# Gate logits of both head halves in one matmul stage from the second batch on, the raw second half kept in SBUF, engine orders rewritten

## Chip, cores and metric

The kernel runs on one core of one Trainium2 chip. The metric is device microseconds (us) from start to end of one execution, as the median of several runs; less is better. In this core TensorE (PE in the profile) does the matmuls and transposes, VectorE (DVE), ScalarE (ACT) and GpSimd (POOL) the elementwise work, and SyncE (SP) issues DMAs. Each of the five works through its own list of instructions in order, and waits on semaphores that the others raise.

## Reference

The input x has 8 batches of 512 tokens of 128 channels. Each batch goes through a half-step feed-forward network (FFN), an attention with 16 heads of 64, and a second half-step FFN, each behind a layernorm and added to its input:

```python
x = x + 0.5 * ffn(layernorm(x)); x = x + attention(layernorm(x)); x = x + 0.5 * ffn(layernorm(x))
# attention, x of (8, 512, 128), H = 16, D = 64
q = rmsnorm((x @ Wq), q_rms_w); k = rmsnorm((x @ Wk), k_rms_w); v = x @ Wv
omega_eff = softplus(omega) * slopes
u_n = u / maximum(norm(u), 1e-6)
gate_logits = einsum('bthd,hd->bht', k, u_n) / sqrt(D)
gate = softplus(gate_logits)
bias = -dist * omega_eff[:, None, None] * gate[:, :, None, :]     # dist = max(i - j, 0), causal
attn = softmax(einsum('bihd,bjhd->bhij', q, k) / sqrt(D) + bias)
y = (attn @ v) @ Wproj
```

The FFN is 128 to 512 to 128 with an exact GELU, and its two weight matrices get a small addition made from the batch's own first tokens, so they are made anew for each batch. What the change is about is one number per token and head, the gate logit. It is linear in k before the RMS norm, so the kernel gets it from the layernormed tokens times a prepared matrix (wu, 128 channels by 16 heads) and divides by the RMS of k afterwards.

## The kernel before, in words

**Precision.** Most matmul operands are fp16 pairs, a high part and a low part. A product (`product`, L1121 to L1125) is three matmuls into one PSUM region: high by high, high by low, low by high.

**Order of the work.** All five engines are driven by one table, `ORDER`: for each engine a list of stages for the parts `lead`, `first` (batch 0), `body` (batches 1 to 6, one list used six times) and `final` (batch 7). A stage in the part of batch b belongs to batch b (THIS), to the one before (LAST) or to the one after (NEXT). So the part of batch b holds its attention beside the first FFN and the projections of the next batch and the second FFN of the one before. The order is written out by hand. Each engine runs its list strictly in order; `run` calls the function that belongs to the stage.

**PSUM.** Four of the eight banks form a ring (banks 4 to 7). Every PE stage takes one or more units of it in the order of PE's own list (`UNITS`: 3 for the max-scores of a head, 2 for two turned heads, 1 for most others, 1 for `gl`). `room` makes PE wait until the bank's last user is done (`work_taken`), `full` makes a reader wait for PE (`work_full`), `taken_by` marks the reader's last instruction as the one that frees the bank.

**The stages of a batch**, with their names in the table and the lines of the matmuls or of the main instruction:

- `zt` transposes z, the layernormed tokens; `ln1`, `ln2` are the layernorm's statistics and its normalization; `m`, `h`, `out` the FFN (weights, hidden, output), `"a"` for the first FFN and `"c"` for the second; `add` adds the FFN's result.
- `qk q t` projects queries and keys of a quarter of the heads (four heads, quarter q of 0 to 3) for token block t. ACT copies the result and its squares out of PSUM (L1007, L1006), DVE sums the squares (L1569), `qkn` is the inverse RMS on ACT (L1018) and the multiply with it on POOL (L878).
- `v j t` projects the values of half j; ACT takes the high part, DVE the low part (L1627).
- `gl hf` (`gate_logits`, L1213) is the gate logits of the eight heads of half hf, for all four token blocks: 4 products of 8 columns, 12 matmuls. There are two such stages per batch: `gl 0` stands after the projections of quarters 0 and 1, `gl 1` near the end of the part. On DVE `take_logits` (L1572) multiplies the bank by the inverse RMS of k (`rs`) into `lg`. On ACT `gate_softplus` (L1038, stage `gate`) takes four small activations of `lg`; it waits until the logits' bank is freed. On POOL `gates` (same stage name, L898) makes the two bias rows of each head from them, `gt`. On PE `gr hf` (`gate_rows`, L1224) turns `gt`, on DVE `take_gate_rows` (L1579, L1586) copies it to `gtt`, and on SP `gd` (`place_gates`, L749, L752) issues two DMAs per quarter that put it into rows of the fp16 operand `qk1`.
- `t p` turns the pair of heads p (L1236: eight fp32 transposes); ACT takes the high parts (L1059), DVE the low parts (L1595). SP places them with DMAs (`rows`, `swap`, `back`).
- `a h` (`max_scores`, L1240 to L1254) computes rough scores of head h, from which DVE takes the row maxima (L1605). It waits for the DMAs of the gate rows and the turned heads of its quarter. `nm q` turns the maxima of a quarter, ACT copies them, SP puts them into a row of `qk1`.
- `s h` (`scores`, L1264, L1280 to L1282) computes the scores, transposed, in banks 0 to 2; ACT takes the exponential (L1084). `pl h` on POOL makes its fp16 low part (L852). In batch 7 (`shared_heads`) DVE makes a share of the low parts (L1518).
- `pv h` (`weighted`, L1285) multiplies by the values in bank 3: 128x65 products, the 65th column being the sum; DVE divides by the sum (`over_sums`, L1616, L1620). `yt p` makes the high and low part of a pair's y on ACT and POOL (L856), and SP issues a transposing DMA; `wp i` projects y (the rows `ps<-wp_h,y_hl`), and DVE adds the attention (`add_attention`).

In the list of a body part the stretch around the seam to the next part is, on PE before: `out c`, `qk 3 3`, `a 5`, `pv 13`, `s 15`, `a 6`, **`gl 1`**, `pv 14`, `a 7`, `t 4`, `wp 2`, `nm 1`, `t 5`, `t 6`, and then in the next part `pv 15`, `t 7`, `s 0`, `v 1 0`, `v 1 1`, **`gr 1`**, `s 1`. The wait on `rs` in `take_logits` needs all four `qkn` of a half, and `qkn 3 1` is one of the last stages of the part, which is where `gl 1` stands.

The functions that the change touches:

Of the kernel before, what the change touches and what calls it, by code (L numbers as in the profile page):

```python
# [6 lines left out]
ALU = mybir.AluOpType  # L7
# [39 lines left out]
            ("s", 7, THIS), ("a", 12, THIS), ("v", 1, 3, THIS), ("pv", 6, THIS), ("zt", "att", NEXT), ("s", 8, THIS),
            ("a", 13, THIS), ("qk", 0, 0, NEXT), ("qk", 0, 1, NEXT), ("qk", 0, 2, NEXT), ("pv", 7, THIS),
            ("v", 0, 0, NEXT), ("qk", 0, 3, NEXT), ("qk", 1, 0, NEXT), ("s", 9, THIS), ("a", 14, THIS),
            ("pv", 8, THIS), ("a", 15, THIS), ("qk", 1, 1, NEXT), ("qk", 1, 2, NEXT), ("qk", 1, 3, NEXT),  # L50
            ("nm", 3, THIS), ("wp", 1, THIS), ("v", 0, 1, NEXT), ("gl", 0, NEXT), ("v", 0, 2, NEXT), ("s", 10, THIS),
# [1611 lines left out]
```

## Time and profile before

| | us |
|---|---|
| median of 3 runs | 756.89 |
| lowest, highest | 756.16, 758.61 |
| the profiled execution, whole | 755.66 |
| its span in the profile | 753.9 |

| engine | busy us | share of the span |
|---|---|---|
| PE | 728.3 | 97% |
| DVE | 653.3 | 87% |
| POOL | 646.7 | 86% |
| ACT | 641.6 | 85% |
| PE weight loads (beside PE's matmuls) | 522.6 | 69% |

PE's granted clock is 1.00 of full speed over the whole span, and DMAs move 80 GB/s on average. All rows of the trace come from one profiled execution. A row of a timeline gives the start, the length, the engine, the line, the operation with its output and inputs, and how many instructions of the same kind follow each other (xN); in brackets stands how long the engine was idle before it and which instruction released it. Matmuls are pipelined: a row's length includes the time in the pipeline, so the distance between the starts of two rows tells more of what one costs than its length. PE being "busy" does not mean that it runs at its peak either.

### The profile page before, as it was taken

How to read it: one execution, taken by the hardware profiler on the slowest of the kernel's cores; microseconds unless marked ns; L12 is line 12 of the kernel's file. 1: busy time of each engine (PE TensorE's matmuls, PEld its weight loads, DVE VectorE, ACT ScalarE, POOL GpSimd, SP SyncE). 2: the span in 40 equal slices, each digit the busy share in tenths (PEclk: the TensorE clock that was granted, in tenths of full speed). 3: DMA queues.
4: the chain of work that ended last, by engine and by line, in shares of the span. 5: the costliest groups of instructions: out<-in, count | busy, mean ns of one | idle time of the engine just before them, and what ended most of it. 6: DMA issues, size and time to landing. Idle time of an engine off the chain costs nothing.

```text
span 753.9 us, 25070 instructions
## 1 busy us (share of the span) xinstructions
PE 728.3 (97%) x9273; PEld 522.6 (69%) x9273; DVE 653.3 (87%) x2126; ACT 641.6 (85%) x1424; POOL 646.7 (86%) x760
## 2 busy tenths in 40 slices
PE   6789999999999999999999999999999999999987
PEld 4347667677767776687667777677776876678765
...
DMA packets 99617, 60.32 MB, mean 80 GB/s; under 512 B 74622, under 2 KB 86400, under 8 KB 99496
## 3 DMA queue, kind: packets, MB, share of 16 engines
...
## 4 chain that ended last, share of the span: by engine, by line
PE 74%; ACT 13%; DVE 8%; issue 3%; POOL 2%; DMA 0%; DVEq 0%; ACTq 0%; POOLq 0%
PE ps L1123 13%; PE ps L1125 13%; PE ps L1124 13%; PE ps L1254 8%; PE ps L1280 8%; PE ps L1281 8%; PE ps L1236 4%; ACT qk L1059 3%; PE ps L1282 3%; ACT pt L1084 2%; DVE maxima L1609 2%; ACT hid L996 2%; PE ps L1140 1%; ACT L996 1%; ACT sq L1006 1%
## 5 line engine op out<-in xcount | busy, mean ns | idle before, releaser
L852 POOL TENSOR_TENSOR pt_l<-pt 128x512 f16<-128x512 f32 x366 | 321.4, 907 | 36.2 <-ACT pt L1084 34.5
L1605 DVE CUSTOM_DVE_ANT_0 masked<-ps,causal_row 128x512 f16<-128x512 f32 x480 | 205.7, 486 | 27.4 <-PE ps L1254 26.5
L1084 ACT ACTIVATE pt<-ps 128x512 f32<-128x512 f32 (+1 forms) x384 | 174.6, 534 | 16.3 <-PE ps L1282 15.5
L1280 PE MATMUL ps<-qk 128*128 128x512 f16 (+3 forms) x512 | 146.7, 300 | 0.0
L1281 PE MATMUL ps<-qk 128*128 128x512 f16 (+3 forms) x512 | 146.5, 299 | 0.0
L878 POOL TENSOR_TENSOR qkn<-qkn,rs 128x512 f32<-128x512 f32 x128 | 130.8, 1050 | 13.5 <-ACT rs L1018 12.9
L1123 PE MATMUL ps<-v_buf,pt 128*128 128x65 f16 x1280 | 129.8, 194 | 2.7 <-DVE ytok L1620 1.6
L1124 PE MATMUL ps<-v_buf,pt 128*128 128x65 f16 x1280 | 129.8, 194 | 0.0
L1125 PE MATMUL ps<-v_buf,pt_l 128*128 128x65 f16 x1280 | 129.6, 194 | 0.0
L1123 PEld LDWEIGHTS ps<-v_buf,pt 128*128 128x128 bf16 x1280 | 118.0, 98 | 8.0 <-issue 4.5
L1124 PEld LDWEIGHTS ps<-v_buf,pt 128*128 128x128 bf16 x1280 | 117.5, 98 | 1.7
L1125 PEld LDWEIGHTS ps<-v_buf,pt_l 128*128 128x128 f16 x1280 | 117.6, 97 | 0.0
L1282 PE MATMUL ps<-causal_t,ident 128*128 128x128 f16 x512 | 105.6, 219 | 0.0
L1254 PE MATMUL ps<-qk 96*128 96x512 f16 (+3 forms) x512 | 96.0, 300 | 2.6 <-ACT qkn L1007 1.6
L1006 ACT ACTIVATE sq<-ps 128x512 f32<-128x512 f32 x128 | 77.6, 606 | 14.4 <-PE ps L1125 13.7
L856 POOL TENSOR_TENSOR ytt<-ytok,ytt 128x512 f16<-128x512 f32 x63 | 74.4, 1181 | 17.9 <-ACT ytt L1099 16.6
L1569 DVE TENSOR_REDUCE ss<-sq 128x8 f32<-128x512 f32 x128 | 82.5, 679 | 2.4 <-ACT sq L1006 2.1
L1007 ACT ACTIVATE qkn<-ps 128x512 f32<-128x512 f32 x128 | 78.3, 612 | 0.0
L1123 PE MATMUL ps<-wqkv_h,zt_h_att 128*128 128x512 f16 x192 | 73.1, 381 | 1.9 <-DVE v_buf L1627 0.9
L1254 PEld LDWEIGHTS ps<-qk 96*128 96x128 f16 x512 | 44.0, 97 | 41.9 <-issue 4.2
L1125 PE MATMUL ps<-wqkv_h,zt_l_att 128*128 128x512 f16 x192 | 72.8, 379 | 0.0
L1124 PE MATMUL ps<-wqkv_l,zt_h_att 128*128 128x512 f16 x192 | 72.8, 379 | 0.0
...
## 6 DMA issues: line engine op xcount, KB each, us to landing
qk<-qk SPq DMA_DIRECT2D x128, 128.0 KB, 2.4
...
qk<-gtt SPq DMA_DIRECT2D x64, 8.0 KB
qk<-nmt SPq DMA_DIRECT2D x64, 2.0 KB
y_hl<-ytt SPq DMA_TRANSPOSE x62, 3.1
```

What stands on the lines that cost most here:

```text
L852: g.tensor_tensor(pt_l[:, h % 2, c], pt[:, h % 2, c], pt_h[:, h % 2, c], ALU.subtract).then_inc(s_pt_l, 1)
L878: g.tensor_tensor(qk, qk, r.unsqueeze(4).broadcast_to([P, 2, 2, 2, D]), ALU.mult).then_inc(s_qkn, 1)
L1006: a.activation(sq[:, blk % 4, :], part.bank(s), ACT.Square).then_inc(s_sq, 1)
L1084: a.activation(pt[:, h % 2, c], ps[:, j, 0:width], ACT.Exp).then_inc(s_exp, 1)
L1123: pe.matmul(dst, ah, bh, start=first, stop=False)
L1124: pe.matmul(dst, ah, bl, start=False, stop=False)
L1125: return pe.matmul(dst, al, bh, start=False, stop=last)
L1254: mm = pe.matmul(dst, q1(h)[0:MROW, ib * P:keys], k1(h)[0:MROW, 0:keys], start=True, stop=by_dve)
L1280: pe.matmul(dst, k1(h)[:, keys], q1(h)[:, kb * P:T], start=True, stop=False)
L1281: pe.matmul(dst, k2(h)[:, keys], q2(h)[:, kb * P:T], start=False, stop=False)
L1282: mm = pe.matmul(dst[:, 0:P], ident16[:, :], causal_t16[:, :], start=False, stop=True)
L1605: ins = d.tensor_tensor_reduce(masked[:, part.unit(s, i)[0], col:col + (ib + 1) * P], part.bank(s, i)[:, col:col + (ib + 1) * P], causal_r ...
```

## The change

**The code.** In batch 0 nothing changes. From batch 1 on `gl 1` is gone from PE's lists. `gl 0` computes the logits of all 16 heads: four products of 16 columns (12 matmuls), whose output is laid out in the bank as two pieces of 8 columns, one in each half of the 64 columns. DVE's `take_logits` for the first half does the multiply as before and then copies the second half's 32 raw columns into a new SBUF tensor `lg_raw`; the copy frees the bank, and DVE waits for it. For the second half it reads `lg_raw` and no bank. A new semaphore `s_lg`, raised by the multiply, takes the place of the freed bank for ACT's `gate_softplus`.

**The orders.** The lists `first`, `body` and `final` of all five engines are rewritten; the `lead` lists are the same. The set of stages is the same but for `gl 1` on PE. In the body the larger moves are:

- PE: `gl 1` goes; `a 5` stands before `pv 13` with `qk 3 3` behind it; `nm 0` moves from before `out c` to after `s 15`; `gr 1` moves from before `s 1` to after `v 1 2`; `a 8` stands behind `s 4`.
- ACT: `gate 1` moves from before `t 4` to the end of the part, after `t 6`; `nm 0` and `qkn 3 1` move behind `s 15`.
- DVE: `gl 1` moves from before `a 7` to after `pv 14`; `gr 1` from before `pv 0` to after `wp 3`.
- POOL: `pl 15` moves before `qkn 3 1`; `pl 14` before `qkn 2 0`; `yt 5` before `pl 13`; `yt 3` before `pl 9`.
- SP: `yt 0` and `yt 5` move ahead, `swap` and `nm` stages behind them; `add c` behind `nm 0`.

In `first`, PE's `v 1 1` moves ahead of `s 2`, `a 14` and `a 15` stand between other projections, and around the sixth max-scores the list reads `pv 13`, `qk 3 2`, `a 5`, `qk 3 3`. In `final`, POOL's `pl 14` moves ahead of `m c`, DVE's `pl 14` ahead of `pv 13`, and PE's `h c` behind `pv 14`.

The diff of the code is whole; of the lists those places are shown on which the prediction rests.

```diff
@@ -420,6 +420,7 @@
         qk1 = sb("qk1", [P, 4, 2, 2, 2, T], F16)
         qk2 = sb("qk2", [P, 4, 4, 2, T], F16)
         lg = sb("lg", [P, TB, HH])
+        lg_raw = sb("lg_raw", [P, TB, HH])
         lga = sb("lga", [P, TB, HH])
         lge = sb("lge", [P, TB, HH])
         lgl = sb("lgl", [P, TB, HH])
@@ -572,6 +573,7 @@
         s_ssl = sem("s_ssl")
         s_rs = sem("s_rs")
         s_qkn = sem("s_qkn")
+        s_lg = sem("s_lg")
         s_lga = sem("s_lga")
         s_lge = sem("s_lge")
         s_lgl = sem("s_lgl")
@@ -1036,7 +1038,10 @@
                                      scale=rstd[n][0:ROWS, 0:1]).then_inc(s_z_h[n], 1)
 
             def gate_softplus(part, s, b, hf):
-                part.taken(act, ("gl", *s[1:]))
+                if b == 0:
+                    part.taken(act, ("gl", *s[1:]))
+                else:
+                    act.wait_ge(s_lg, (b - 1) * 2 + hf + 1)
                 a.activation(lga[:, :, :], lg[:, :, :], ACT.Abs, scale=1.0 / W_UP).then_inc(s_lga, 1)
                 act.wait_ge(s_lga, b * 2 + hf + 1)
                 a.activation(lge[:, :, :], lga[:, :, :], ACT.Exp, scale=-1.0).then_inc(s_lge, 1)
@@ -1213,12 +1218,17 @@
             def gate_logits(part, s, b, hf):
                 if b == 0:
                     pe.wait_ge(s_prepared, hf + 1)
-                w = slice(hf * HH, (hf + 1) * HH)
                 part.room(pe, s)
                 for t in range(TB):
                     c = slice(t * P, (t + 1) * P)
-                    mm = product(part.bank(s)[:, t * HH:(t + 1) * HH], zt_h["att"][:, c], zt_l["att"][:, c], wu_h[:, w],
-                                 wu_l[:, w])
+                    if b == 0:
+                        w = slice(hf * HH, (hf + 1) * HH)
+                        mm = product(part.bank(s)[:, t * HH:(t + 1) * HH], zt_h["att"][:, c], zt_l["att"][:, c], wu_h[:, w],
+                                     wu_l[:, w])
+                    else:
+                        both = part.bank(s)[:, 0:2 * TB * HH].rearrange("p (f t n) -> p f t n", f=2, t=TB)[:, :, t, :]
+                        mm = product(both, zt_h["att"][:, c], zt_l["att"][:, c], wu_h[:, :].rearrange("p (f n) -> p f n", f=2),
+                                     wu_l[:, :].rearrange("p (f n) -> p f n", f=2))
                 part.filled_by(mm, s)
 
             def gate_rows(part, s, b, hf):
@@ -1570,11 +1580,22 @@
                                 ALU.add).then_inc(s_sqsum, 1)
 
             def take_logits(part, s, b, hf):
-                part.full(dve, s)
+                if b == 0 or hf == 0:
+                    part.full(dve, s)
+                    raw = part.bank(s)[:, 0:TB * HH]
+                else:
+                    raw = lg_raw[:, :, :].rearrange("p t n -> p (t n)")
                 dve.wait_ge(s_rs, (b * 2 + hf + 1) * 4)
-                part.taken_by(d.tensor_tensor(lg[:, :, :].rearrange("p t (i q n) -> p (t i) q n", q=2, n=2),
-                                              part.bank(s)[:, 0:TB * HH].rearrange("p (t q n) -> p t q n", q=2, n=2),
-                                              rs[:, 1, :, :, :].rearrange("p q t (i n) -> p (t i) q n", n=2), ALU.mult), s)
+                ins = d.tensor_tensor(lg[:, :, :].rearrange("p t (i q n) -> p (t i) q n", q=2, n=2),
+                                      raw.rearrange("p (t q n) -> p t q n", q=2, n=2),
+                                      rs[:, 1, :, :, :].rearrange("p q t (i n) -> p (t i) q n", n=2), ALU.mult)
+                if b == 0:
+                    part.taken_by(ins, s)
+                    return
+                ins.then_inc(s_lg, 1)
+                if hf == 0:
+                    part.taken_by(d.tensor_copy(lg_raw[:, :, :].rearrange("p t n -> p (t n)"), part.bank(s)[:, TB * HH:2 * TB * HH]), s)
+                    part.taken(dve, s)
 
             def take_gate_rows(part, s, b, hf):
                 part.full(dve, s)
```

PE's lists (end of `first`, end of `body`, `final` before its last stages):

```diff
-            ("a", 4, NEXT), ("s", 14, THIS), ("nm", 0, NEXT), ("qk", 3, 1, NEXT), ("qk", 3, 2, NEXT),
-            ("qk", 3, 3, NEXT), ("a", 5, NEXT), ("s", 15, THIS), ("a", 6, NEXT), ("wp", 2, THIS), ("gl", 1, NEXT),
-            ("a", 7, NEXT), ("t", 4, NEXT), ("pv", 14, THIS), ("nm", 1, NEXT), ("t", 5, NEXT), ("t", 6, NEXT),
...
+            ("pv", 12, THIS), ("a", 3, NEXT), ("qk", 3, 0, NEXT), ("s", 14, THIS), ("a", 4, NEXT), ("qk", 3, 1, NEXT),
+            ("pv", 13, THIS), ("qk", 3, 2, NEXT), ("a", 5, NEXT), ("qk", 3, 3, NEXT), ("nm", 0, NEXT),
+            ("pv", 14, THIS), ("a", 6, NEXT), ("s", 15, THIS), ("a", 7, NEXT), ("t", 4, NEXT), ("wp", 2, THIS),
+            ("nm", 1, NEXT), ("t", 5, NEXT), ("t", 6, NEXT),
...
-            ("qk", 3, 1, NEXT), ("qk", 3, 2, NEXT), ("nm", 0, NEXT), ("out", "c", LAST), ("qk", 3, 3, NEXT),
-            ("a", 5, NEXT), ("pv", 13, THIS), ("s", 15, THIS), ("a", 6, NEXT), ("gl", 1, NEXT), ("pv", 14, THIS),
-            ("a", 7, NEXT), ("t", 4, NEXT), ("wp", 2, THIS), ("nm", 1, NEXT), ("t", 5, NEXT), ("t", 6, NEXT),
+            ("qk", 3, 1, NEXT), ("qk", 3, 2, NEXT), ("out", "c", LAST), ("a", 5, NEXT), ("pv", 13, THIS),
+            ("qk", 3, 3, NEXT), ("a", 6, NEXT), ("s", 15, THIS), ("nm", 0, NEXT), ("pv", 14, THIS), ("a", 7, NEXT),
+            ("t", 4, NEXT), ("wp", 2, THIS), ("nm", 1, NEXT), ("t", 5, NEXT), ("t", 6, NEXT),
         ],
...
-            ("pv", 12, THIS), ("s", 14, THIS), ("pv", 13, THIS), ("s", 15, THIS), ("h", "c", LAST), ("pv", 14, THIS),
+            ("pv", 12, THIS), ("s", 14, THIS), ("pv", 13, THIS), ("s", 15, THIS), ("pv", 14, THIS), ("h", "c", LAST),
```

ACT's list, the end of the body:

```diff
-            ("qk", 2, 3, NEXT), ("qkn", 2, 0, NEXT), ("qk", 3, 0, NEXT), ("s", 14, THIS), ("qk", 3, 1, NEXT),
-            ("qk", 3, 2, NEXT), ("qkn", 2, 1, NEXT), ("nm", 0, NEXT), ("qk", 3, 3, NEXT), ("qkn", 3, 0, NEXT),
-            ("qkn", 3, 1, NEXT), ("s", 15, THIS), ("gate", 1, NEXT), ("t", 4, NEXT), ("yt", 6, THIS), ("nm", 1, NEXT),
-            ("t", 5, NEXT), ("t", 6, NEXT),
...
+            ("qk", 2, 3, NEXT), ("s", 14, THIS), ("qk", 3, 0, NEXT), ("qkn", 2, 0, NEXT), ("qk", 3, 1, NEXT),
+            ("qk", 3, 2, NEXT), ("qkn", 2, 1, NEXT), ("qkn", 3, 0, NEXT), ("qk", 3, 3, NEXT), ("s", 15, THIS),
+            ("nm", 0, NEXT), ("yt", 6, THIS), ("qkn", 3, 1, NEXT), ("t", 4, NEXT), ("nm", 1, NEXT), ("t", 5, NEXT),
+            ("t", 6, NEXT), ("gate", 1, NEXT),
```

DVE's list, the body's start and end and a place in `final`:

```diff
-            ("pv", 15, LAST), ("t", 7, THIS), ("ln1", "a", NEXT), ("v", 1, 0, THIS), ("ln2", "a", NEXT),
-            ("v", 1, 1, THIS), ("gr", 1, THIS), ("pv", 0, THIS), ("v", 1, 2, THIS), ("wp", 3, LAST),
+            ("pv", 15, LAST), ("t", 7, THIS), ("ln1", "a", NEXT), ("ln2", "a", NEXT), ("v", 1, 0, THIS),
+            ("v", 1, 1, THIS), ("pv", 0, THIS), ("wp", 3, LAST), ("gr", 1, THIS), ("v", 1, 2, THIS),
...
-            ("qk", 3, 3, NEXT), ("pv", 13, THIS), ("a", 6, NEXT), ("gl", 1, NEXT), ("a", 7, NEXT), ("t", 4, NEXT),
-            ("wp", 2, THIS), ("pv", 14, THIS), ("t", 5, NEXT), ("t", 6, NEXT),
...
+            ("qk", 3, 0, NEXT), ("qk", 3, 1, NEXT), ("qk", 3, 2, NEXT), ("add", "c", LAST), ("a", 5, NEXT),
+            ("pv", 13, THIS), ("qk", 3, 3, NEXT), ("a", 6, NEXT), ("a", 7, NEXT), ("t", 4, NEXT), ("wp", 2, THIS),
+            ("pv", 14, THIS), ("gl", 1, NEXT), ("t", 5, NEXT), ("t", 6, NEXT),
...
-            ("pl", 13, THIS), ("pv", 12, THIS), ("pv", 13, THIS), ("pl", 14, THIS), ("wp", 1, THIS), ("pl", 15, THIS),
+            ("pl", 13, THIS), ("pv", 12, THIS), ("pl", 14, THIS), ("pv", 13, THIS), ("wp", 1, THIS), ("pl", 15, THIS),
```

POOL's list, the end of the body and a place in `final`, and SP's body:

```diff
-            ("pl", 11, THIS), ("m", "c", LAST), ("pl", 12, THIS), ("h", "c", LAST), ("yt", 4, THIS), ("pl", 13, THIS),
-            ("yt", 5, THIS), ("qkn", 2, 0, NEXT), ("pl", 14, THIS), ("qkn", 2, 1, NEXT), ("qkn", 3, 0, NEXT),
-            ("qkn", 3, 1, NEXT), ("pl", 15, THIS), ("yt", 6, THIS), ("gate", 1, NEXT),
...
+            ("pl", 11, THIS), ("m", "c", LAST), ("pl", 12, THIS), ("h", "c", LAST), ("yt", 4, THIS), ("yt", 5, THIS),
+            ("pl", 13, THIS), ("pl", 14, THIS), ("qkn", 2, 0, NEXT), ("qkn", 2, 1, NEXT), ("qkn", 3, 0, NEXT),
+            ("pl", 15, THIS), ("qkn", 3, 1, NEXT), ("yt", 6, THIS), ("gate", 1, NEXT),
...
-            ("pl", 12, THIS), ("pl", 13, THIS), ("yt", 5, THIS), ("m", "c", LAST), ("pl", 14, THIS), ("yt", 6, THIS),
...
+            ("pl", 12, THIS), ("pl", 13, THIS), ("yt", 5, THIS), ("pl", 14, THIS), ("m", "c", LAST), ("yt", 6, THIS),
...
-            ("ln1", "a", NEXT), ("yt", 7, LAST), ("rows", 2, THIS), ("gd", 2, THIS), ("swap", 2, THIS),
-            ("yt", 0, THIS), ("yt", 1, THIS), ("rows", 3, THIS), ("gd", 3, THIS), ("back", 2, THIS),
-            ("swap", 3, THIS), ("nm", 2, THIS), ("nm", 3, THIS), ("back", 3, THIS), ("yt", 2, THIS), ("yt", 3, THIS),
-            ("rows", 0, NEXT), ("gd", 0, NEXT), ("rows", 1, NEXT), ("swap", 0, NEXT), ("swap", 1, NEXT),
-            ("gd", 1, NEXT), ("yt", 4, THIS), ("back", 0, NEXT), ("add", "c", LAST), ("nm", 0, NEXT), ("yt", 5, THIS),
-            ("back", 1, NEXT), ("nm", 1, NEXT), ("yt", 6, THIS),
+            ("ln1", "a", NEXT), ("yt", 7, LAST), ("rows", 2, THIS), ("gd", 2, THIS), ("yt", 0, THIS),
+            ("swap", 2, THIS), ("yt", 1, THIS), ("gd", 3, THIS), ("rows", 3, THIS), ("swap", 3, THIS),
+            ("back", 2, THIS), ("nm", 2, THIS), ("back", 3, THIS), ("yt", 2, THIS), ("yt", 3, THIS), ("nm", 3, THIS),
+            ("rows", 0, NEXT), ("gd", 0, NEXT), ("rows", 1, NEXT), ("gd", 1, NEXT), ("swap", 0, NEXT),
+            ("yt", 4, THIS), ("yt", 5, THIS), ("swap", 1, NEXT), ("back", 0, NEXT), ("back", 1, NEXT),
+            ("nm", 0, NEXT), ("add", "c", LAST), ("nm", 1, NEXT), ("yt", 6, THIS),
```

## Rows read from the trace of the kernel before

**Rows 1.** The page, part 1: busy us, share of the span, instructions.

```profile
PE 728.3 (97%) x9273; PEld 522.6 (69%) x9273; DVE 653.3 (87%) x2126; ACT 641.6 (85%) x1424; POOL 646.7 (86%) x760
```

**Rows 2.** Windows: stretch, its us, busy us of each engine (instructions), clock, DMA share, GB/s.

```profile
459.80:548.50 88.70, 88.34 (x1149) 64.07 (x1148) 77.16 (x263) 79.23 (x179) 81.12 (x93) 1.00 0.36 80
455.50:476.50 21.00, 20.77 (x244) 14.52 (x242) 17.86 (x45) 20.74 (x47) 20.40 (x25) 1.00 0.41 92
490.00:504.50 14.50, 14.38 (x204) 11.37 (x202) 14.19 (x43) 11.57 (x30) 11.91 (x16) 1.00 0.40 82
```

**Rows 3.** Timeline of PE, seam of a middle batch: start us, us, engine, line, form.

```profile
495.01 0.86 PE L1254 MATMUL ps<-qk 96*128 96x512 f16 x4
495.78 1.18 PE L1236 MATMUL ps<-ident,qkn 128*128 128x128 f32 x8
497.08 0.22 PE L1123 MATMUL ps<-wp_h,y_hl 128*128 128x128 f16 x1
...
501.28 1.07 PE L1236 MATMUL ps<-ident,qkn 128*128 128x128 f32 x8
```

**Rows 4.** Groups by line and form: busy us, mean ns of one | idle before.

```profile
L1123 PE MATMUL ps<-wu_h,zt_h_att 128*128 128x8 f16 x64 | 6.4, 168 | 1.1 <-POOL wu_l L896 1.1
...
L1123 PEld LDWEIGHTS ps<-wu_h,zt_h_att 128*128 128x128 f16 x64 | 5.4, 96 | 2.3 <-POOL wu_l L896 1.3 <-ACT qkn L1007 0.2
```

**Rows 5.** Timeline of PE, the gate-logits stage of batch 7 and what follows.

```profile
671.25 0.17 PE L1123 MATMUL ps<-wu_h,zt_h_att 128*128 128x8 f16 x1
...
671.55 0.19 PE L1123 MATMUL ps<-v_buf,pt 128*128 128x65 f16 x1
671.58 0.19 PE L1124 MATMUL ps<-v_buf,pt 128*128 128x65 f16 x1
```

**Rows 6.** Groups by line and form, DVE's copy out of PSUM.

```profile
L1586 DVE COPY gtt<-ps 128x128 f16<-128x128 f16 x16 | 3.5, 218 | 0.8 <-PE ps L1227 0.7
```

**Rows 7.** Timeline of DVE behind the first gate multiply of batch 5.

```profile
465.46 0.75 DVE L1595 SCALAR_TENSOR_TENSOR qk<-ps,qws,qk 128x512 f16<-128x512 f32 x1 [0.20 <-ACT qk L1059]
```

**Rows 8.** Timeline of DVE, seam of batch 5.

```profile
491.01 0.69 DVE L1605 CUSTOM_DVE_ANT_0 masked<-ps,causal_row 128x512 f16<-128x512 f32 x1 [0.17 <-PE ps L1254]
...
495.45 0.18 DVE L1575 TENSOR_TENSOR lg<-ps,rs 128x32 f32<-128x32 f32 x1
495.55 0.68 DVE L1605 CUSTOM_DVE_ANT_0 masked<-ps,causal_row 128x512 f16<-128x512 f32 x1
```

**Rows 9.** Timeline of ACT: first turned head of a part; gate of a seam.

```profile
413.25 0.69 ACT L1059 ACTIVATE qk<-ps,qws 128x512 f16<-128x512 f32 x1 [0.41 <-PE ps L1236]
...
495.67 0.23 ACT L1040 ACTIVATE lga<-lg 128x32 f32<-128x32 f32 x1 [0.49 <-DVE lg L1575]
...
496.45 0.69 ACT L1059 ACTIVATE qk<-ps,qws 128x512 f16<-128x512 f32 x1
```

**Rows 10.** Timeline: SP's gate-row DMAs; PE's max-scores that need them.

```profile
508.69 1.45 SPq L752 DMA_DIRECT2D qk<-gtt  x2
...
514.40 0.71 PE L1254 MATMUL ps<-qk 96*128 96x512 f16 x4
```

**Rows 11.** Timeline of PE, sixth max-scores of batch 1.

```profile
136.13 0.28 PE L1254 MATMUL ps<-qk 96*128 96x256 f16 x1 [0.86 <-ACT qkn L1007]
```

**Rows 12.** Timeline of POOL, DVE, PE in the last part.

```profile
725.34 1.04 POOL L861 TENSOR_TENSOR w_l<-weff 128x512 f16<-128x512 f32 x1
...
727.45 2.51 POOL L852 TENSOR_TENSOR pt_l<-pt 128x512 f16<-128x512 f32 x2
...
728.68 3.13 DVE L1518 TENSOR_TENSOR pt_l<-pt 128x512 f16<-128x512 f32 x3
...
730.21 0.19 PE L1123 MATMUL ps<-v_buf,pt 128*128 128x65 f16 x1 [0.54 <-POOL pt_l L852]
...
732.50 0.19 PE L1123 MATMUL ps<-v_buf,pt 128*128 128x65 f16 x1 [1.23 <-DVE ytok L1620]
```

**Rows 13.** Timeline of PE, output projection in batch 2.

```profile
242.92 0.22 PE L1123 MATMUL ps<-wp_h,y_hl 128*128 128x128 f16 x1 [0.64 <-issue]
```

More of the change, by code:

```diff
@@ L47 @@
[L47 to L51, printed above, removed]
@@ L65 @@
-            ("a", 10, THIS), ("wp", 0, THIS), ("pv", 4, THIS), ("a", 11, THIS), ("out", "a", NEXT), ("nm", 2, THIS),
+            ("pv", 15, LAST), ("t", 7, THIS), ("s", 0, THIS), ("v", 1, 0, THIS), ("v", 1, 1, THIS), ("s", 1, THIS),
+            ("v", 1, 2, THIS), ("gr", 1, THIS), ("s", 2, THIS), ("pv", 0, THIS), ("wp", 3, LAST), ("zt", "a", NEXT),
+            ("pv", 1, THIS), ("s", 3, THIS), ("m", "a", NEXT), ("s", 4, THIS), ("pv", 2, THIS), ("a", 8, THIS),
+            ("v", 1, 3, THIS), ("pv", 3, THIS), ("a", 9, THIS), ("s", 5, THIS), ("h", "a", NEXT), ("s", 6, THIS),
@@ new lines @@
+            ("s", 9, THIS), ("qkn", 0, 1, NEXT), ("qk", 1, 2, NEXT), ("qk", 1, 3, NEXT), ("qkn", 1, 0, NEXT),
+            ("v", 0, 1, NEXT), ("qkn", 1, 1, NEXT), ("v", 0, 2, NEXT), ("nm", 3, THIS), ("gate", 0, NEXT),
+            ("s", 10, THIS), ("t", 0, NEXT), ("t", 1, NEXT), ("s", 11, THIS), ("v", 0, 3, NEXT), ("t", 2, NEXT),
+            ("t", 3, NEXT), ("qk", 2, 0, NEXT), ("yt", 4, THIS), ("qk", 2, 1, NEXT), ("s", 12, THIS),
+            ("qk", 2, 2, NEXT), ("qkn", 2, 0, NEXT), ("s", 13, THIS), ("yt", 5, THIS), ("qk", 2, 3, NEXT),
@@ L125 @@
+            ("qk", 3, 0, NEXT), ("qkn", 2, 1, NEXT), ("s", 14, THIS), ("qk", 3, 1, NEXT), ("qk", 3, 2, NEXT),
+            ("qkn", 3, 0, NEXT), ("qk", 3, 3, NEXT), ("yt", 6, THIS), ("qkn", 3, 1, NEXT), ("nm", 0, NEXT),
+            ("s", 15, THIS), ("t", 4, NEXT), ("nm", 1, NEXT), ("t", 5, NEXT), ("t", 6, NEXT), ("gate", 1, NEXT),
         ],
         "body": [
-            ("t", 7, THIS), ("yt", 7, LAST), ("s", 0, THIS), ("v", 1, 0, THIS), ("v", 1, 1, THIS), ("s", 1, THIS),
+            ("t", 7, THIS), ("yt", 7, LAST), ("s", 0, THIS), ("v", 1, 0, THIS), ("s", 1, THIS), ("v", 1, 1, THIS),
@@ new lines @@
+            ("v", 0, 0, NEXT), ("nm", 3, THIS), ("qkn", 1, 0, NEXT), ("v", 0, 1, NEXT), ("qkn", 1, 1, NEXT),
+            ("v", 0, 2, NEXT), ("m", "c", LAST), ("gate", 0, NEXT), ("t", 0, NEXT), ("t", 1, NEXT), ("s", 11, THIS),
+            ("t", 2, NEXT), ("s", 12, THIS), ("v", 0, 3, NEXT), ("t", 3, NEXT), ("h", "c", LAST), ("yt", 4, THIS),
+            ("yt", 5, THIS), ("qk", 2, 0, NEXT), ("qk", 2, 1, NEXT), ("s", 13, THIS), ("qk", 2, 2, NEXT),
+            ("qk", 2, 3, NEXT), ("s", 14, THIS), ("qk", 3, 0, NEXT), ("qkn", 2, 0, NEXT), ("qk", 3, 1, NEXT),
@@ L193 @@
+            ("ln2", "c", LAST), ("wp", 0, THIS), ("add", "a", NEXT), ("ln1", "att", NEXT), ("pv", 5, THIS),
+            ("zt", "c", LAST), ("ln2", "att", NEXT), ("pv", 6, THIS), ("a", 12, THIS), ("zt", "att", NEXT),
             ("pv", 7, THIS), ("a", 13, THIS), ("a", 14, THIS), ("qk", 0, 0, NEXT), ("qk", 0, 1, NEXT),
-            ("qk", 0, 2, NEXT), ("a", 15, THIS), ("qk", 0, 3, NEXT), ("pv", 8, THIS), ("qk", 1, 0, NEXT),
+            ("qk", 0, 2, NEXT), ("pv", 8, THIS), ("a", 15, THIS), ("qk", 0, 3, NEXT), ("qk", 1, 0, NEXT),
@@ L200 @@
[L200 to L202 removed]
+            ("wp", 1, THIS), ("pv", 10, THIS), ("t", 2, NEXT), ("gr", 0, NEXT), ("v", 0, 3, NEXT), ("t", 3, NEXT),
+            ("pv", 11, THIS), ("a", 0, NEXT), ("a", 1, NEXT), ("a", 2, NEXT), ("a", 3, NEXT), ("qk", 2, 0, NEXT),
```

171 lines of the change are left out of this document (78 added, 93 removed).

## Prediction

> **What bounds the kernel now.** I read the page's busy shares first: TensorE (PE) is busy 97% of a span of 753.9 us, the other engines 85 to 87% [rows 1]. The reader is to see that no second engine is full over the whole span, so the next question is where PE is not. The table of windows answers it [rows 2]. One middle batch takes 88.70 us and PE is busy 88.34 us of it; the six middle batches repeat this. Inside the batch there are two places where another engine is full. From 455.5 to 476.5 ScalarE (ACT) is busy 20.74 of 21.00 us. From 490.0 to 504.5, which I call the seam (end of one part of the order, start of the next), VectorE (DVE) is busy 14.19 of 14.50 us. So a microsecond taken off PE is worth a microsecond only where PE leads; in these two places it is worth what the other engine also gives up.
>
> The removed stage lies in the seam. There PE is late although its row shows no idle time: eight fp32 transposes have 1.07 us at 501.28 but 1.18 us at 495.78, and the next stage starts only 1.30 us after 495.78; the max-scores ahead of them stretch to 0.86 us [rows 3]. I count about 0.7 us of such hidden waiting on DVE per seam.
>
> **Part 1, the products.** Per batch from the second on, the second gate-logits stage goes: 12 matmuls of 8 columns, each with its weight load, seven times, 84 in all. A row of such a matmul shows 168 ns and its load 96 ns [rows 4], but these overlap. The distance in the timeline counts: the first starts at 671.25 and the next stage at 671.55, so 12 take 0.30 us, 25 ns each [rows 5]. 7 x 0.30 = **2.1 us** off PE. The Trainium skill ("TensorE: Matmul & The Clock Gate", section "Back-to-back issue gap") says that in a stream of LDWEIGHTS and MATMUL pairs both set the spacing, about 81 ns at 128 columns; by that 84 x 0.081 = 6.8 us would go. The rows show 25 ns with a load ahead of each, so I keep 2.1.
>
> The remaining stage's matmuls become 16 columns wide. No row has 16; 8 columns stand 25 ns apart and 65 columns 29 to 30 ns (671.55, 671.58) [rows 5], so 12 x 7 of them add 0 to 0.4 us; nearest is 8, and I take 0. The output's two pieces of 8 columns have no row; as 8 contiguous columns already run at the same distance I price the stride at nothing, with the same upper end.
>
> **Part 2, DVE.** Seven PSUM copies of 128x32 are new, with a wait of DVE for its own copy. The nearest row is the 128x128 copy, 218 ns [rows 6]; with the hand-over 0.2 to 0.3 us per batch. Queued behind it are the value low part and the head's division, and ACT and PE wait for these. What covers it: at the next low part, 1.4 us later, DVE waits 0.20 us for ACT [rows 7], about the copy's length. I take 0 on the path; with the cover gone it costs 7 x 0.3 = 2.1 us. The second half's multiply reads SBUF instead of PSUM; same size, price 0 (at most 0.1 us each way). ACT's gate of the first half is released by the multiply, not by the bank, so the copy does not delay it.
>
> **Part 3, the seam of the body.** DVE's gate multiply leaves the place before the last max-scores; it holds the stream 0.10 us there (495.45 to 495.55). The max-scores of head 5 (heads count from 0, as in the table), which open the stretch, now follow PE's FFN output directly, with one projection and one turn of maxima moved behind it, about 0.7 us earlier on PE; DVE waited 0.17 us for them [rows 8]. So DVE gives up 0.27 us where PE gives up 0.30. That is the amount that lets PE's saving through, and no more: I take 0.3 us per batch, already in the 2.1. The bank of the removed stage is not a further gain, since the moved turn of maxima takes its place in the ring between the same neighbours. GpSimd (POOL) now does the last normalization behind head 15's three low parts; it has time for that, because a y low part moves ahead into a stretch before head 13 in which it stood idle.
>
> The gate's four ACT operations move behind the last turned heads, before the next part's first ones. They hold ACT 0.78 us (495.67 to 496.45); ACT waits 0.41 us for PE at the new place (413.25) [rows 9]. So up to 0.37 us per seam may fall on the chain turned head, y high part, exponentials of head 0 of the next part; PE has two value stages to do before the scores that need them. I take 0, upper end 7 x 0.37 = 2.6 us.
>
> The gate rows follow later too: DVE copies them behind the attention add, and SyncE's (SP) two DMAs of gate rows, now at 508.69, go out about 2.8 us later. The max-scores that need them start at 514.40 [rows 10] and move behind one score stage (1.3 us). A pair of such DMAs takes 1.45 us to issue; they must have landed by 515.7. With the queue's next rows (transposes, swaps, placements) reordered but none added or removed, I take 0. SP's other moves put the y transposes ahead of waits for maxima rows: no new DMA, earlier landings.
>
> **Part 4, the first part (batches 0 and 1).** PE idles 0.86 us inside the max-scores of head 5, on a bank that ACT must empty [rows 11]. The new order puts a head's values and one projection on either side of it, so the bank asked for is two projections older. DVE has to follow, so of 0.86 I take **0.8 us**; bounds 0 and 1.3.
>
> **Part 5, the last part.** POOL computes the FFN's weight low parts (2.1 us from 725.34) before head 14's low part (727.45), for which PE idles 0.54 us at 730.21; then DVE does three low parts (3.13 us from 728.68) and PE idles 1.23 us until 732.50 [rows 12]. The new order puts head 14 first on POOL, its DVE share before the division of head 13, and the hidden stage (12 x 0.22 us on PE) after head 14's values. Then head 14 can start some 2 us earlier and the hidden stage fills the wait for head 15. What is late next is DVE's three low parts: they can start about 1 us earlier. Gain **1.0 us**, bounds 0 and 1.5.
>
> **Sum.** 2.1 + 0.8 + 1.0 = 3.9 us. Against the profiled execution (755.66 us, span 753.9 and 1.76 around it) that is 751.8. That execution lies 1.2 us under the median of 756.89; the same distance on top gives **752.9 us**. Part of the distance may be landings: in one batch PE idles 0.64 us at 242.92 for a late y transpose that no other batch waits for [rows 13]. The measurement can tell about 0.3%, 2.3 us, from no change: faster means under 754.6, slower over 759.2.
>
> **Rivals.**
> A. Only the products pay (chance 0.20): the two places of parts 4 and 5 find another wait. 756.89 - 2.1 = 754.8, within 0.3%. For it: in both places another engine is close behind.
> B. ACT and DVE eat the saving (0.06): the copies' 0.3 us and the gate's 0.37 us land in front of a full stretch. 756.89 - 3.9 + up to 4.2 gives 757. For it: both engines' full stretches [rows 2]; against: the waits in [rows 7, 9].
> C. Slower (0.09): the gate rows arrive late. The mechanism sits in SP's queue: its gate-row DMAs wait for a DVE copy that now waits for the attention add, which waits for a y transpose. It decides once they land over about 1 us later than I count; each further microsecond holds head 8's max-scores by as much, in seven batches. At 1 us: 756.89 - 3.9 + 7 = 760. A single late landing as at 242.92 then costs twice, on PE and again on the queue.
> D. Weight loads are PE's real limit (0.02): 84 x 96 ns = 8.1 us go instead of 2.1, so 746.9; against it stand the distances of [rows 5]. This is the skill's rule with this kernel's load time.
> E. The change doesn't do what it says (0.01): the code keeps 12 matmuls per batch and drops 84; 756.9.
>
> **How the numbers follow.** The forecast has 0.62. With D, and a third of A's cases falling under 754.6, faster is 0.70; the rest of A, B and E give 0.21; C gives 0.09. The range starts at 750.2 (upper bounds of parts 4 and 5, 1.0 us together, and 1.7 us less waiting at late landings) and ends at 756.5 (A with the 16-column cost of 0.4 and half of the gate's 2.6); it leaves out C, D and most of B.
>
> **What the next profile would show.** Twelve 16-column products that take 0.30 us together; in the group of L1123 with wu_h, 8 matmuls of 8 columns and 28 of 16 where 64 of 8 stood. Middle batches of 88.4 us. No 0.86 us wait in the first part; head 15's values start about 1 us after the hidden stage ends at most. Wrong if middle batches stay at 88.7 us (B), if SP's gate rows land after PE has finished head 4's scores (C), or if DVE shows a new wait behind the copy.

## The result and the profile after

The changed kernel takes 761.09 us (median of 8 runs, 759.15 to 762.30), the one before 757.00 us (8 runs, 755.26 to 758.61). The ratio is 1.0054, 95% interval 1.0040 to 1.0067: slower by 4 us, where I had forecast 4 us less. The profiled execution took 759.48 us, its span is 757.7 us against 753.9.

The page's first part, with the first line of the page (span and instructions), answers to [rows 1]:

```profile
span 757.7 us, 24914 instructions
...
PE 729.8 (96%) x9189; PEld 520.0 (69%) x9189; DVE 655.3 (86%) x2133; ACT 644.3 (85%) x1424; POOL 647.0 (85%) x760
```

84 matmuls are gone and seven DVE copies have come, as the code says. Where the time came from is told by the starts of PE's stages. Between the start of the first part and that of the first body lie 78.1 us in both kernels. The six bodies (the parts of batches 1 to 6) take 536.1 us where they took 533.0, and the last part is 0.5 us longer; the lead is 0.2 us longer. So 3.1 of the 3.8 us stand in the bodies, that is, in what I had priced at a gain of 0.3 us each. A body in the table of windows (columns as in [rows 2]):

```profile
592.06:681.13 89.07, 88.46 (x1138) 63.72 (x1136) 77.44 (x263) 79.54 (x180) 81.31 (x92) 1.00 0.40 80
```

PE is busy 88.46 us in it, more than the 88.34 us of the longer list of work before [rows 2]: its waits hide in the rows' lengths. They are seen in the distances of the starts. The new body on PE, some 15 us in: max-scores of head 8, then the projection v 1 3, then head 9:

```profile
607.53 0.71 PE L1264 MATMUL ps<-qk 96*128 96x512 f16 x4
608.33 0.39 PE L1128 MATMUL ps<-wqkv_h,zt_h_att 128*128 128x512 f16 x1
...
609.90 0.91 PE L1264 MATMUL ps<-qk 96*128 96x512 f16 x4
```

The projection starts 0.80 us after head 8; the four matmuls need 0.55 us (the same pair in an experiment below). Head 9's four stretch to 0.91 us. A third such place, 0.30 us, is ahead of wp 0. All three starts come 0.06 to 0.16 us after the end of a DVE instruction: DVE is late. Its own timeline shows why. First the kernel before, then the changed one, from the layernorm statistics of the next batch on:

```profile
594.81 0.66 DVE L1627 TENSOR_TENSOR v_buf<-ps,v_buf 128x512 f16<-128x512 f32 x1
596.65 0.16 DVE L1447 TENSOR_REDUCE shift_a<-mv_a 128x4 f32<-128x8 f32 x1 [1.18 <-ACT mv_a L1024]
...
597.93 0.18 DVE L1616 RECIPROCAL rden<-ps 128x4 f32<-128x4 f32 x1 [0.38 <-PE ps L1125]
...
599.28 0.69 DVE L1561 SCALAR_TENSOR_TENSOR x<-ps,x_att 128x512 f32<-128x512 f32 x1
600.00 0.81 DVE L1452 TENSOR_TENSOR z_hl<-z_a,z_hl 32x128 f16<-32x128 f32 x1
```

```profile
597.48 0.87 DVE L1437 BATCH_NORM_STATS2 stats_a<-x_in 128x6 f32<-128x128 f32 x4 [1.12 <-DMA x_in<-in_L_attn_x]
...
599.63 0.16 DVE L1457 TENSOR_REDUCE shift_a<-mv_a 128x4 f32<-128x8 f32 x1 [0.87 <-ACT mv_a L1026]
599.71 1.29 DVE L1648 TENSOR_TENSOR v_buf<-ps,v_buf 128x512 f16<-128x512 f32 x2
...
602.28 0.69 DVE L1571 SCALAR_TENSOR_TENSOR x<-ps,x_att 128x512 f32<-128x512 f32 x1 [0.70 <-PE ps L1130]
603.00 0.23 DVE L1607 COPY gtt<-ps 128x128 f16<-128x128 f16 x1
603.15 0.68 DVE L1648 TENSOR_TENSOR v_buf<-ps,v_buf 128x512 f16<-128x512 f32 x1
603.86 0.94 DVE L1462 TENSOR_TENSOR z_hl<-z_a,z_hl 32x128 f16<-32x128 f32 x1
```

From the shift (L1447, now L1457) to the split of the first rows of z (L1452, now L1462) DVE takes 3.35 us before and 4.23 us after; 0.66 us of the difference is the low part of v 1 0, which before filled a part of the wait for ACT. In the new list it waits 0.70 us for PE's wp 3 while the copy of the gate rows and the low part of v 1 2, 0.9 us together, stand behind that wait. So there are three candidates: this wait, the wait for ACT with the low part of v 1 0 now behind it, and the x load, for which DVE waits 1.12 us where it waited 0.22 us.

### The profile page after: what moved, and what is told of

Read it like the earlier page. It is cut to its first block, busy times and chain, and to the rows that moved or that the text cites. A ratio compares the mean times of both kernels' runs of the same rounds, so it can differ in the third digit from the quotient of the medians.

```text
span 757.7 us, 24914 instructions
## 1 busy us (share of the span) xinstructions
PE 729.8 (96%) x9189; PEld 520.0 (69%) x9189; DVE 655.3 (86%) x2133; ACT 644.3 (85%) x1424; POOL 647.0 (85%) x760
## 4 chain that ended last, share of the span: by engine, by line
PE 62%; DVE 17%; ACT 10%; issue 4%; POOL 3%; DMA 2%; SPq 1%; DVEq 0%; ACTq 0%; POOLq 0%
PE ps L1128 12%; PE ps L1130 11%; PE ps L1129 11%; PE ps L1264 6%; PE ps L1290 6%; PE ps L1291 6%; PE ps L1246 6%; DVE masked L1626 4%; PE ps L1292 2%; ACT qk L1064 2%; ACT hid L998 2%; DVE pt_l L1528 2%; DVE maxima L1630 2%; ACT pt L1089 1%; ACT L998 1%
## 5 line engine op out<-in xcount | busy, mean ns | idle before, releaser
L1264 PE MATMUL ps<-qk 96*128 96x512 f16 (+3 forms) x512 | 98.0, 300 | 2.0 <-ACT qkn L1009 0.7
L1009 ACT ACTIVATE qkn<-ps 128x512 f32<-128x512 f32 x128 | 78.1, 610 | 0.0
```

The costliest lines, as they stand in the source:

```text
L1264: mm = pe.matmul(dst, q1(h)[0:MROW, ib * P:keys], k1(h)[0:MROW, 0:keys], start=True, stop=by_dve)
```

## The experiments

All but the last (parts_alone3) are made on a form of the two kernels in which the transposing DMA of y is replaced by plain ones, so that y is not transposed and the output is not the reference's. The counts of the waits on it are adapted, nothing else.

```diff
-                sp.dma_start_transpose(...)...then_inc(s_y_turned[p % 2], 16)
+                for i in range(2):
+                    sp.dma_start(y_end[0][:, i, :] if last else y_hl[:, p % 2, i, :], ytt[:, p % 2, i, :]).then_inc(s_y_turned[p % 2], 16)
```

**Base (w_before).** 

> The kernel before, with each transposing DMA of y (256 KB) replaced by two plain DMAs of 128 KB, so y is left untransposed and the output is not the reference's; every wait stands. It is the base for the other kernels with the same replacement (all named w_). A plain 128 KB DMA lands 2.4 us after its issue and takes about 0.6 us to issue, two of them about 3.0 us where the transposing one takes 3.1. Expected: within 1 us of the kernel before, 757 us.

**The changed kernel on it (w_after).** 

> The changed kernel with plain DMAs for y. If the replacement keeps what matters, it is 3.5 to 4.5 us slower than w_before. If the loss hangs on the transposing DMAs alone, it is as fast as w_before or faster.

Ratios here and below are to the kernel before as it is, run beside each of them. The rows come from three chips, so they are compared by their ratios, not by their medians:

| kernel | median us | ratio | 95% interval | span of the profile |
|---|---|---|---|---|
| w_before | 756.26 | 0.9999 | 0.9989 to 1.0008 | 754.0 |
| w_after | 760.07 | 1.0063 | 1.0049 to 1.0077 | 757.0 |
| w_code | 757.58 | 1.0013 | 1.0002 to 1.0023 | 754.5 |
| w_mid | 761.68 | 1.0077 | 1.0064 to 1.0090 | 759.5 |
| w_start | 757.07 | 0.9994 | 0.9982 to 1.0005 | 755.4 |
| w_start_mid | 757.09 | 1.0002 | 0.9991 to 1.0014 | 753.4 |
| w_start_a | 759.79 | 1.0056 | 1.0042 to 1.0070 | 759.9 |
| w_start_b | 755.80 | 1.0008 | 0.9996 to 1.0019 | 753.6 |
| w_best | 757.89 | 1.0010 | 0.9999 to 1.0022 | 754.7 |
| w_last | 757.58 | 1.0012 | 1.0001 to 1.0023 | 756.9 |

The replacement keeps the effect: the loss is there with plain DMAs, and in the sixth body PE's new waits stand at the same stages with the same lengths. The transposing DMAs are not its main cause. In the bodies, though, w_after is 2.2 us behind w_before (535.4 and 533.2 us), where the changed kernel is 3.1 us behind. Two of its bodies, the third and the fifth, are 0.3 and 0.5 us longer than the shortest ones; there PE waits at the scores of head 8 (idle 0.36 us at 537.66) for SP's DMA of the maxima rows. In w_after the same two bodies are within 0.1 us of the shortest. That share was not taken apart further.

**The code alone (w_code).** 

> All lists as before, only gl 1 taken out of PE's; the code of the change (16-column products, copy to lg_raw, s_lg); plain DMAs for y. Theory O (the rewritten orders cost, the code pays): the seven parts shrink by 0.24 us of PE work each, 1.7 us, and stall as before: w_before - 1.7 us. Rival K (the copy and the new wait on VectorE cost): w_before or slower, with new idle time on PE behind gl 0's copy, at the projections and turned heads that follow it.

```diff
-            ("a", 5, NEXT), ("pv", 13, THIS), ("s", 15, THIS), ("a", 6, NEXT), ("gl", 1, NEXT), ("pv", 14, THIS),
+            ("a", 5, NEXT), ("pv", 13, THIS), ("s", 15, THIS), ("a", 6, NEXT), ("pv", 14, THIS),
```

Both theories missed: no gain, no wait behind the copy. One body of w_before, then of w_code:

```profile
411.75:500.47 88.72, 88.34 (x1150) 64.06 (x1148) 77.19 (x262) 79.32 (x180) 81.13 (x93) 1.00 0.30 80
```

```profile
411.77:500.48 88.71, 88.23 (x1138) 63.83 (x1136) 77.28 (x263) 79.31 (x180) 81.12 (x93) 1.00 0.30 80
```

The stage is gone and the body is as long. In the seam PE now waits 0.27 us ahead of pv 14 and 0.44 us at t 4, where 0.22 us stood at t 4 and 0.15 us at a 7. DVE's timeline there, from the maxima of head 5 to the low parts of t 4, has one idle time, at its start:

```profile
580.17 0.69 DVE L1626 CUSTOM_DVE_ANT_0 masked<-ps,causal_row 128x512 f16<-128x512 f32 x1 [0.17 <-PE ps L1264]
...
582.62 0.42 DVE L1641 TENSOR_TENSOR ytok<-ps,rden 128x256 f32<-128x256 f32 x1
...
584.60 0.18 DVE L1589 TENSOR_TENSOR lg<-lg_raw,rs 128x32 f32<-128x32 f32 x1
...
586.35 0.75 DVE L1616 SCALAR_TENSOR_TENSOR qk<-ps,qws,qk 128x512 f16<-128x512 f32 x1
```

The seam's length is DVE's 6.2 us of work, so 0.3 us of PE work in it is worth nothing. In its first part w_code waits 1.76 us at t 4, where w_before waits 0.35 us: the lists of before had gl 1 there, ahead of a 7. That makes its first part 1.0 us longer than the base's, more than the 0.5 us by which its whole profile is longer.

**The middle of the body put back (w_mid).** 

> The changed kernel with plain DMAs for y and one stretch of the body's lists put back as before: from m a to out c's successor out a on PE, with ACT's and DVE's lists of that stretch. Theory O names three new waits of PE for VectorE there (0.26 us before v 1 3, 0.19 at a 9, 0.30 at wp 0, in each of six bodies) and one of 0.19 us that came back: w_after - 3.3 us, and PE goes from a 10 to wp 0 without the 0.3 us. Rival S (the loss is at the seam and at landings): w_after within 1 us.

On PE (ACT's and DVE's lists of the stretch go with it):

```diff
-            ("pv", 1, THIS), ("s", 3, THIS), ("m", "a", NEXT), ("s", 4, THIS), ("pv", 2, THIS), ("a", 8, THIS),
-            ("v", 1, 3, THIS), ("pv", 3, THIS), ("a", 9, THIS), ("s", 5, THIS), ("h", "a", NEXT), ("s", 6, THIS),
+            ("pv", 1, THIS), ("s", 3, THIS), ("m", "a", NEXT), ("pv", 2, THIS), ("a", 8, THIS), ("s", 4, THIS),
+            ("pv", 3, THIS), ("v", 1, 3, THIS), ("s", 5, THIS), ("a", 9, THIS), ("h", "a", NEXT), ("s", 6, THIS),
...
```

It became slower still. PE's waits at v 1 3, a 9 and wp 0 are gone and one of 1.06 us stands at pv 2, in every body:

```profile
607.77 0.19 PE L1128 MATMUL ps<-v_buf,pt 128*128 128x65 f16 x1 [0.88 <-POOL pt_l L854]
```

The profile names POOL's low part, but the bank of pv 2 has to be emptied by DVE's division of pv 1 first, and that ends last, 0.15 us before the start:

```profile
607.20 0.42 DVE L1641 TENSOR_TENSOR ytok<-ps,rden 128x256 f32<-128x256 f32 x1
```

So the new middle of PE's list was an answer to a late DVE, not the cause. That gave the next theory: the head of DVE's list.

**DVE's head put back (w_start), and with the middle (w_start_mid).** 

> w_after with one edit: the head of VectorE's body list is v 1 0 before ln2 a and v 1 2, gr 1 before pv 0 and wp 3 again (work that is ready ahead of work that waits). New theory D: in the changed list two waits of VectorE, for ScalarE's inverse root (0.91 us) and for PE's wp 3 (0.70 us), stand ahead of value low parts that are ready, so VectorE comes about 0.9 us later to pv 1's division and to m a, and PE waits 0.27 us at v 1 3 and 0.18 us at a 9 in each body. With the edit these two waits go: w_after - 2.7 us. If the gap is made by the late x load alone (rival X), w_after within 0.5 us.

> w_start with the stretch of w_mid put back too. Theory D: PE's wait of 1.06 us at pv 2, which made w_mid slower than w_after, is VectorE's lateness, so it falls to about 0.2 us: w_mid - 5.2 us, near w_before. Rival X (x load) or a late low part on GpSimd: w_mid within 1 us, the wait stays.

```diff
-            ("pv", 15, LAST), ("t", 7, THIS), ("ln1", "a", NEXT), ("ln2", "a", NEXT), ("v", 1, 0, THIS),
-            ("v", 1, 1, THIS), ("pv", 0, THIS), ("wp", 3, LAST), ("gr", 1, THIS), ("v", 1, 2, THIS),
+            ("pv", 15, LAST), ("t", 7, THIS), ("ln1", "a", NEXT), ("v", 1, 0, THIS), ("ln2", "a", NEXT),
+            ("v", 1, 1, THIS), ("v", 1, 2, THIS), ("gr", 1, THIS), ("pv", 0, THIS), ("wp", 3, LAST),
```

These two lines of one engine's list take back the whole loss: from 1.0063 to 0.9994. The waits at v 1 3 and a 9 are gone, the one at wp 0 stays. In w_start_mid the wait at pv 2 is 0.20 us and the ratio 1.0002. The size was larger than I expected for w_start (5.2 us by the ratios, 2.7 expected); its profile has 1.6 us, part of it hidden by a lead that is 0.7 us slower (granted clock 0.97 in its first 64 us, 1.00 in w_after's); its six bodies take 2.3 us less than w_after's.

**Which of the two moves (w_start_a, w_start_b).** 

> w_after with one swap in VectorE's body list: v 1 0 ahead of ln2 a. w_start, with this swap and the next, took back 5 us. In the trace of w_after VectorE waits 1.0 us for ScalarE's inverse root at ln2 a, with the low part of v 1 0 (0.66 us) ready behind it. If that wait is the cause, nearly all of it comes back here: w_after - 4 us, w_start_b within 1 us of w_after.

> w_after with one move in VectorE's body list: v 1 2 and gr 1 ahead of pv 0 and wp 3. In the trace of w_after VectorE waits 0.7 us for PE at wp 3, with the gate rows' copy and the low part of v 1 2 (0.9 us together) behind it. If that wait is the cause, nearly all of the 5 us comes back here, w_after - 4 us; if each wait has its share, each kernel gets 2 to 3 us back.

w_start_a has v 1 0 ahead of ln2 a and is as slow as w_after; its six bodies take 535.4 us, as w_after's do. The low part fills a piece of the wait for ACT (0.62 us is left of 1.03 us), but DVE then waits 0.53 us more for PE at pv 0, and the 0.70 us at wp 3 stay. w_start_b has v 1 2 and gr 1 ahead of pv 0 and wp 3 and is level with the kernel before. A body of it, and DVE at the same place:

```profile
588.50:677.00 88.50, 88.00 (x1138) 63.91 (x1137) 77.28 (x263) 79.30 (x179) 81.22 (x92) 1.00 0.30 80
```

```profile
593.50 0.87 DVE L1437 BATCH_NORM_STATS2 stats_a<-x_in 128x6 f32<-128x128 f32 x4 [0.74 <-DMA x_in<-in_L_attn_x]
...
596.08 0.16 DVE L1457 TENSOR_REDUCE shift_a<-mv_a 128x4 f32<-128x8 f32 x1 [1.30 <-ACT mv_a L1026]
596.16 1.89 DVE L1648 TENSOR_TENSOR v_buf<-ps,v_buf 128x512 f16<-128x512 f32 x3
597.97 0.21 DVE L1607 COPY gtt<-ps 128x128 f16<-128x128 f16 x1
...
598.75 0.69 DVE L1571 SCALAR_TENSOR_TENSOR x<-ps,x_att 128x512 f32<-128x512 f32 x1
599.47 0.78 DVE L1462 TENSOR_TENSOR z_hl<-z_a,z_hl 32x128 f16<-32x128 f32 x1
```

Shift to z: 3.39 us, the wait for wp 3 has been filled by ready work. The wait for ACT (1.30 us) and the one for x (0.74 us) are still there and cost nothing, so the late x load is ruled out as the cause. The edit moves two operations, and the runs do not tell which of them matters more. On PE head 8 and v 1 3 now stand 0.55 us apart:

```profile
603.88 0.71 PE L1264 MATMUL ps<-qk 96*128 96x512 f16 x4
604.43 0.38 PE L1128 MATMUL ps<-wqkv_h,zt_h_att 128*128 128x512 f16 x1
```

**A wait that only moved (w_best).** 

> w_start_mid with gl 0 ahead of v 0 2 on PE, as it stands on VectorE. That takes away PE's wait of 0.26 us at t 1 in six bodies: w_start_mid - 1.5 us, and below w_before by about 1 us.

```diff
-            ("v", 0, 1, NEXT), ("v", 0, 2, NEXT), ("gl", 0, NEXT), ("s", 11, THIS), ("t", 0, NEXT), ("t", 1, NEXT),
+            ("v", 0, 1, NEXT), ("gl", 0, NEXT), ("v", 0, 2, NEXT), ("s", 11, THIS), ("t", 0, NEXT), ("t", 1, NEXT),
```

The wait at t 1 (0.26 us) went, and one of 0.30 us came at v 0 2, one stage earlier. It is another bank's: with the swap v 0 2 comes four ring units behind nm 3 and needs the bank from which ACT copies the maxima until 640.10, 0.05 us before v 0 2 starts; at t 1 it had been the bank of v 0 2, which DVE's low part holds. No gain, and no version here beats the kernel before.

**The last part alone (w_last), and its operations by themselves (parts_alone3).** 

> w_before with three swaps in the last part alone: GpSimd's pl 14 ahead of m c, VectorE's pl 14 ahead of pv 13, PE's h c behind pv 14 (part 5 of my forecast, there -1.0 us). Now expected: pv 14 comes 2 us sooner, but the low parts of head 15 on VectorE stretch to 3.6 us beside GpSimd's (a low part took 0.69 us alone on VectorE and 1.41 us beside GpSimd), so pv 15 starts no sooner: w_before within 0.3 us.

```diff
-            ... ("s", 15, THIS), ("h", "c", LAST), ("pv", 14, THIS),
+            ... ("s", 15, THIS), ("pv", 14, THIS), ("h", "c", LAST),
-            ("pl", 13, THIS), ("pv", 12, THIS), ("pv", 13, THIS), ("pl", 14, THIS), ("wp", 1, THIS), ("pl", 15, THIS),
+            ("pl", 13, THIS), ("pv", 12, THIS), ("pl", 14, THIS), ("pv", 13, THIS), ("wp", 1, THIS), ("pl", 15, THIS),
-            ... ("yt", 5, THIS), ("m", "c", LAST), ("pl", 14, THIS), ("yt", 6, THIS),
+            ... ("yt", 5, THIS), ("pl", 14, THIS), ("m", "c", LAST), ("yt", 6, THIS),
```

No gain here, against the 1.0 us of my forecast, and the intervals do not exclude a loss of 1 us. The three low parts of head 15 on DVE, and PE at pv 15 behind them:

```profile
729.49 4.05 DVE L1518 TENSOR_TENSOR pt_l<-pt 128x512 f16<-128x512 f32 x3 [0.69 <-PE ps L1125]
```

```profile
734.23 0.19 PE L1123 MATMUL ps<-v_buf,pt 128*128 128x65 f16 x1 [2.19 <-DVE ytok L1620]
```

They took 3.13 us in [rows 12] and 3.69 us in the changed kernel. In this profile pv 15 starts 7.9 us after head 15's scores, 6.9 us in w_before, so 1.0 us is lost where I expected none: the three low parts start 3.1 us after these scores, as before, and not 2.5 us as in the changed kernel. Why they start no sooner here is not shown.

> Only two things are measured, the rest of the computation is left out (the output is x). First the low part of the exponentials (128x512 fp16 <- fp32, bf16), four times on VectorE alone, then on VectorE and GpSimd at once: in the last part of the changed kernel three on VectorE took 3.69 us beside GpSimd's weight low parts, in the one before 3.13 us. If the two engines hold each other up, one takes some 0.9 us alone on either and 1.1 us or more together; if not, the same. Then the products of the gate logits, in rows of 96 matmuls of 8 columns, of 16 contiguous ones and of 16 in two pieces of 8. In the kernels 12 take 0.30 us at 8 columns and about 0.31 at 16 in two pieces. If the 16 columns cost what is lost between my 2.1 and the 1.7 us seen, they stand 5 ns further apart than the 8; if the column count costs nothing, all three stand 25 ns apart.

The starts of the low parts stand 0.72 us apart on DVE alone and 1.44 us while POOL does the same; on POOL 1.12 us alone and 1.44 us together. The rows of DVE alone and together (four, eight):

```profile
10.45 2.87 DVE L70 TENSOR_TENSOR lo<-pt 128x512 f16<-128x512 f32 x4 [6.85 <-DMA buf<-in_L_attn_x]
17.97 11.68 DVE L75 TENSOR_TENSOR lo<-pt 128x512 f16<-128x512 f32 x8 [4.64 <-POOL lo L84]
```

The products: starts 25.2 ns apart at 8 columns, 25.2 ns at 16 contiguous ones, 26.5 ns at 16 in two pieces of 8.

## Why the prediction was wrong, point by point

Stretch by stretch: the bodies were to give 1.8 us and cost 3.1, the first part was to give 1.1 and gave nothing, the last part was to give 1.0 and cost 0.5. The bodies decide, so part 3 does. Two sums are off, without weight: 756.89 - 3.9 is 753.0, and the upper price of rival B is 2.1 + 2.6 = 4.7 us, not 4.2. The idle time of [rows 13], which I put down to a late y transpose, stands at the same place with 0.35 us in w_before, which has no transposing DMA; so that was not its only cause.

**Part 1, the products: right.** In the changed kernel the twelve of 16 columns take 0.30 us, as the twelve of 8 did [rows 5]:

```profile
643.20 0.17 PE L1128 MATMUL ps<-wu_h,zt_h_att 128*128 128x16 f16 x1
...
643.50 0.38 PE L1290 MATMUL ps<-qk 128*128 128x512 f16 x1
```

Seven removed stages are 2.1 us of PE work, and the two pieces cost 12 x 1.3 ns, 0.02 us a batch. Rival D (weight loads at 96 ns) is out: 96 such matmuls in a row, each with its load, stand 25 ns apart. The 81 ns that the Trainium skill gives ("TensorE: Matmul & The Clock Gate", section "Back-to-back issue gap") are for 128 columns and do not carry over. At 128 columns the trace does not agree with them either: the matmuls of the output projection, each with its own load, start 56 ns apart:

```profile
242.92 0.22 PE L1123 MATMUL ps<-wp_h,y_hl 128*128 128x128 f16 x1 [0.64 <-issue]
242.98 0.22 PE L1124 MATMUL ps<-wp_l,y_hl 128*128 128x128 f16 x1
243.03 0.22 PE L1125 MATMUL ps<-wp_h,y_hl 128*128 128x128 f16 x1
```

**Part 2, the copy: right in the bodies.** w_code shows no new wait behind it there. In its first part t 0, which follows soon behind gl 0, takes 0.20 us longer than in w_before; whether the copy is the reason is not shown.

**Part 3, the seam: wrong, and the step that failed first.** I let the 2.1 us through because DVE would give up 0.27 us in the same stretch. w_code shows that PE's 0.3 us alone are worth nothing there: its DVE list keeps the gate multiply in the seam. With the new lists, in the changed kernel, PE waits 0.25 us at a 6 and 0.25 us at t 4 in the seam where it waited 0.15 us at a 7 and 0.22 us at t 4, so about half of the 0.30 us came through.

**Part 3, the head of the next part: wrong, and the costly step.** I followed gr 1 behind the attention add and asked only what this does to the gate rows, as rival C did. They were not late: PE has no wait at a 8. What I did not price, and so put at nothing, is that DVE's wait at wp 3 now had ready DVE work behind it. That alone is 3.0 us over the six bodies (535.4 us in w_after, 532.4 us in w_start_b; body 6 takes 89.1 and 88.5 us) and made the sign. Without it an undisturbed body is 0.2 us shorter than in w_before (88.5 and 88.7 us), and the whole is level with the kernel before. Rival C, 9 in 100, named the right instruction, the attention add ahead of the gate rows' copy, with the wrong consequence; that its 760 us lies near the measured 761.09 is luck. The gate's move on ACT made POOL idle 2.2 us ahead of the gate, in place of 2.5 us behind it; the low parts of head 0 start 4.9 us after PE's first stage of the part in w_before and 4.8 us in w_after, so it cost nothing.

**Part 4, the first part: wrong.** PE's wait of 0.86 us [rows 11] became one of 0.63 us idle at the next projection, on the same bank user (ACT qkn). On PE, from the start of head 5's max-scores to the next stage, 1.58 us became 1.34. So 0.2 of the 0.8 us came. The rest of it and the 0.3 us of the removed stage went into waits elsewhere in the part. The part is 78.1 us as before.

```profile
136.09 0.39 PE L1128 MATMUL ps<-wqkv_h,zt_h_att 128*128 128x512 f16 x1 [0.63 <-ACT qkn L1009]
```

**Part 5, the last part: mechanism half right, gain nil.** In the changed kernel pv 14 starts 2.1 us after head 15's scores began, 4.6 us before. DVE's three low parts do start 0.5 us earlier, where I had said about 1, and take 0.56 us longer:

```profile
731.93 3.69 DVE L1528 TENSOR_TENSOR pt_l<-pt 128x512 f16<-128x512 f32 x3
```

So pv 15 starts 6.9 us after head 15's scores in both. I had treated the durations as fixed while I moved POOL's work beside them. The 0.5 us that the last part became longer lies ahead of these scores, which start 48.3 us after the part's first stage in place of 47.8. The stages at the start of that list were rewritten too, and no run took them apart.
